# A second buffer for normed key tiles, first and last tile normed by halves, turns and scores placed inside the next batch's first product

## The reference, cut to what matters

```python
kvx = jnp.einsum('bsi,oi->bso', cond, w_kv_x)
kx, vx = jnp.split(kvx, 2, axis=-1)
kx = _ln(kx.reshape(b, sc, g, d), kxln_w, kxln_b)      # mean and variance over d = 128
vx = vx.reshape(b, sc, g, d)
xout = _gqa(qx, kx, vx).reshape(b, s, nh * d)          # softmax(qx kx / sqrt(d)) vx
```

## Time and profile before

| | |
|---|---|
| median of 3 runs | 2918.24 us (2917.55 to 2921.14) |
| the profiled execution | 2916.87 us, span of its instructions 2915.1 us |
| mean granted TensorE clock | 0.969 of full |
| busy over the span | PE 92%, PEld 75%, DVE 61%, ACT 52%, POOL 16% |

### The profile page before, as it was taken

How to read it: one execution, slowest core, us unless ns; L and a number is a source line. 1 busy time by engine, 2 the same in 40 slices (tenths; PEclk the granted TensorE clock), 3 DMA queues, 4 the chain that set the end, 5 groups by cost and what they waited for, 6 DMA issues and landing times.

```text
span 2915.1 us, 38394 instructions
## 1 busy us (share of the span) xinstructions
PE 2690.7 (92%) x13446; PEld 2184.2 (75%) x13446; DVE 1785.1 (61%) x4709; ACT 1503.8 (52%) x2907; POOL 462.5 (16%) x376
## 2 busy tenths in 40 slices
PE   6869999999999999999999999989998889868999
PEld 5767778778787787787787786768876678756887
DVE  6745536537437447356356366568768776557997
ACT  6934424425326336235244344336675467846776
POOL 3401102002002002011011020004332222011111
PEclk9978999999999999999999999999999899988999
DMA  3425002002012011021020021335666542529996
GB/s 119 131 73 184 25 8 88 11 24 81 2 42 63 3 56 48 4 70 32 5 79 23 9 82 42 101 140 148 178 182 174 137 104 58 176 87 386 373 372 238
DMA packets 247006, 303.07 MB, mean 104 GB/s; under 512 B 144024, under 2 KB 165144, under 8 KB 233504
## 3 DMA queue, kind: packets, MB, share of 16 engines
q1 hardware_dynamic: 244016, 296.36, 32.0%
q0 software_dynamic: 2800, 4.27, 0.6%
HBM read 259.48 MB, written 46.98 MB: 105 GB/s over the span
## 4 chain that ended last, share of the span: by engine, by line
PE 75%; DVE 11%; ACT 6%; DMA 3%; issue 2%; SPq 2%; POOL 1%; POOLq 0%; DVEq 0%; ACTq 0%
PE ps L103 18%; PE ps L105 18%; PE ps L104 18%; PE ps L734 5%; PE ps L716 3%; PE ps L753 3%; PE ps L783 2%; DVE lnw L1958 1%; DVE zz L1961 1%; DVE cv L1925 1%; PE ps L774 1%; POOL lnw L1080 1%; DVE lnw L831 1%; DMA ca<-cat_d 1%; PE ps L481 1%
## 5 line engine op out<-in xcount | busy, mean ns | idle before, releaser
L1080 POOL TENSOR_TENSOR lnw<-lnw,half 128x8 f32<-128x8 f32 (+1 forms) x104 | 170.7, 1642 | 1451.5 <-DVE lnw L836 1451.5
L103 PE MATMUL ps<-cnh,pth 128*128 128x512 f32 (+1 forms) x832 | 332.5, 400 | 13.6 <-ACT kn L962 13.6
L103 PE MATMUL ps<-whf,cth 128*128 128x512 f32 (+1 forms) x832 | 336.7, 405 | 6.9 <-DVE ctl L538 3.5
L105 PE MATMUL ps<-whf,ctl 128*128 128x512 f32 (+1 forms) x832 | 327.5, 394 | 0.0
L104 PE MATMUL ps<-wlf,cth 128*128 128x512 f32 (+1 forms) x832 | 327.0, 393 | 0.0
L105 PE MATMUL ps<-cnh,ptl 128*128 128x512 f32 (+1 forms) x832 | 326.6, 392 | 0.0
L104 PE MATMUL ps<-cnl,pth 128*128 128x512 f32 (+1 forms) x832 | 326.4, 392 | 0.0
L962 ACT ACTIVATE pr<-ps,lnw 128x128 f32<-128x128 f32 (+1 forms) x384 | 144.6, 457 | 164.0 <-DVE lnw L855 164.0
L2399 DVE TENSOR_TENSOR ml<-mr,mh 128x2048 fp32r<-128x2048 f32 x90 | 203.5, 2288 | 32.4 <-ACT mh L2343 32.4
L952 DVE TENSOR_SCALAR pc<-ps,sm 128x512 f32<-128x512 f32 x64 | 48.1, 751 | 283.6 <-PE ps L105 283.6
L1024 ACT ACTIVATE xo<-ps 128x128 f32<-128x128 f32 x64 | 17.8, 278 | 370.7 <-PE ps L783 370.7
(11 more groups left out here) (332 smaller groups left out, 6103.3 us busy)
## 6 DMA issues: line engine op xcount, KB each, us to landing
mr<-in_moe SPq DMA_DIRECT2D x90, 1024.0 KB, 6.8
ctr<-in_ctxt SPq DMA_DIRECT2D x96, 256.0 KB, 2.9
pr<-in_ctxn SPq DMA_DIRECT2D x96, 256.0 KB
wr<-in_wqkv SPq DMA_DIRECT2D x64, 256.0 KB, 2.9
wvf<-in_wattn SPq DMA_DIRECT2D x12, 1024.0 KB, 5.0
ca<-cat_d SPq DMA_DIRECT2D x16, 512.0 KB, 4.1
qk_d<-cv SPq DMA_DIRECT2D x32, 256.0 KB, 3.2
wr<-in_wz SPq DMA_DIRECT2D x32, 256.0 KB, 3.1
```

What stands on the lines that cost most here:

```text
L103: pe.matmul(dst, lh, rh, start=first, stop=False)
L105: return pe.matmul(dst, ll, rh, start=False, stop=last)
L1080: po.tensor_tensor(rs[0:w, s, :], nv[0:w, s, :], half[0:w, 0:8], ALU.pow).then_inc(kx_rs, 1)
```

## The change

- `kn` and `kn0` now alternate: odd tiles go to `kn`, even ones to `kn0` (`kn_of`), and `kn_free` waits for the turn of the tile before the last.
- Tiles 0 and 12 of a batch are treated by halves of 4 heads: TensorE reports the first part of the product (`kx_half`), VectorE takes the statistics of each half by itself, GpSimd makes two powers of 4 columns for them.
- `nmr` is made of heads 0 to 3 only, those that ScalarE norms (`kx_nmr_dv`).
- A turn waits for ScalarE's heads before its first four transposes and for VectorE's before the other four, instead of for both before the first.
- On TensorE the turn of tile 10 moves between the two parts of tile 12's product, and the turn of tile 12 and the last score piece move into the first part of the next batch's tile 0; the turn of tile 12 lay ahead of it.
- On VectorE, step i does the norm of tile i-2, the split `cnl` of tile i-1, then the statistics of tile i-1. At the batch's end the order is: statistics of tile 12, first half; norm of 11; `nmr` of 12; second half; `cnl` of 11; norm of 12. The first-half statistics of the next tile 0 come right behind the softmax's maximum.
- On ScalarE the norm of tile 12 comes ahead of the copies `kf` of tile 11.

```diff
@@
+        def in_halves(n):
+            return n % 13 in (0, 12)
+        def kn_of(n):
+            return kn if n % 13 % 2 else kn0
...
@@ kx_pe
                 elif i == 0:
                     pe.wait_ge(kn_ac, n)
-                    pe.wait_ge(kn_dv, n)
...
             for part in parts:
+                if part == 1 and i == 0 and b > 0:
+                    pe.wait_ge(kn_dv, n)
                 for c in chunks:
...
+                if part == 0 and chunks[-1] == 3 and in_halves(n):
+                    f.then_inc(kx_half, 1)
@@ kx_turn_pe
-            src = kn if i else kn0
-            pe.wait_ge(kn_ac, n + 1)
-            pe.wait_ge(kn_dv, n + 1)
+            src = kn_of(n)
             for p in range(2):
+                pe.wait_ge((kn_ac, kn_dv)[p], n + 1)
@@ s3_pe
-                    kx_pe(pe, n)
+                    kx_pe(pe, n, (0,))
+                    if i == 12:
+                        kx_turn_pe(pe, n - 2)
+                    kx_pe(pe, n, (1,))
...
-                    if i > 1:
+                    if 1 < i < 12:
                         kx_turn_pe(pe, n - 2)
                 kx_turn_pe(pe, 13 * b + 11)
                 for w in range(3):
                     score_pe(pe, b, 0, w)
+                if b + 1 < NB:
+                    kx_pe(pe, 13 * b + 13, (0,), (0, 1))
                 kx_turn_pe(pe, 13 * b + 12)
                 if b + 1 < NB:
-                    kx_pe(pe, 13 * b + 13, (0,), (0, 1))
+                    kx_pe(pe, 13 * b + 13, (0,), (2, 3))
                 score_pe(pe, b, 0, 3)
                 if b + 1 < NB:
-                    kx_pe(pe, 13 * b + 13, (0,), (2, 3))
                     kx_pe(pe, 13 * b + 13, (1,))
@@ kn_free
             elif i > 1:
-                eng.wait_ge(k_turned, 2 * (n - 1) + 2)
+                eng.wait_ge(k_turned, 2 * (n - 2) + 2)
+
+        def kx_nmr_dv(dv, n):
+            i = n % 13
+            w, s = TILES[i][1], i % 4
+            dv.wait_ge(kx_rs, kx_stat_of(n, 0))
+            dv.scalar_tensor_tensor(nmr[0:w, s, 0:4], mv[0:w, s, 0:4, 0], -1.0, rs[0:w, s, 0:4],
+                                    ALU.mult, ALU.mult).then_inc(kx_nm, 1)
@@ s3_dv
                     n = 13 * b + i
+                    if i > 2:
+                        kx_norm_dv(dv, n - 2)
+                    if i < 12:
+                        split_ctxn_dv(dv, n - 1)
                     if i > 1:
                         kx_stats_dv(dv, n - 1)
-                    if i > 2:
-                        kx_norm_dv(dv, n - 2)
-                    split_ctxn_dv(dv, n - 1)
                     if i + 2 < 13 or (i == 11 and b + 1 < NB):
                         split_ctxt_dv(dv, n + 2)
+                kx_stats_dv(dv, 13 * b + 12, (0,))
                 kx_norm_dv(dv, 13 * b + 11)
-                kx_stats_dv(dv, 13 * b + 12)
+                kx_nmr_dv(dv, 13 * b + 12)
+                kx_stats_dv(dv, 13 * b + 12, (1,))
+                split_ctxn_dv(dv, 13 * b + 11)
                 kx_norm_dv(dv, 13 * b + 12)
...
+                if b + 1 < NB:
+                    kx_stats_dv(dv, 13 * b + 13, (0,))
                 t_rinv = {0: rinv_dv(dv, b, 0)}
                 split_ctxn_dv(dv, 13 * b + 12)
...
                     if g == 0 and b + 1 < NB:
-                        kx_stats_dv(dv, 13 * b + 13)
+                        kx_stats_dv(dv, 13 * b + 13, (1,))
+                        kx_nmr_dv(dv, 13 * b + 13)
                     p_low_dv(dv, b, g, (0, 1))
@@ s3_ac
                 kx_norm_ac(ac, 13 * b + 11)
+                kx_norm_ac(ac, 13 * b + 12)
                 k_out_ac(ac, 13 * b + 11)
-                kx_norm_ac(ac, 13 * b + 12)
                 k_out_ac(ac, 13 * b + 12)
```

More of the change, by code:

```diff
@@ L588, in s1b_ac @@
                     split_ctxt_ac(ac, 1)
+        kx_half = sem("kx_half")
         kx_done, kx_var, kx_rs, kx_nm = sem("kx_done"), sem("kx_var"), sem("kx_rs"), sem("kx_nm")
@@ L599, in p_exp_of, with kx_half_of, kx_stat_of @@
             return m + 1 + (m + 7) // 8
+        def in_halves(n):
+            return n % 13 in (0, 12)
+        def kx_half_of(n):
+            return 2 * (n // 13) + 1 + n % 13 // 12
+        def kx_stat_of(n, h):
+            b, i = divmod(n, 13)
+            return 15 * b + (1 + h if i == 0 else i + 2 + (h if i == 12 else 0))
+        def kn_of(n):
+            return kn if n % 13 % 2 else kn0
         KSET = [(0, 2, 6)[(i + 2) % 3] for i in range(13)]
@@ L823, in s3_pe, with kx_stats_dv @@
                         xo_pe(pe, m - 1)
-        def kx_stats_dv(dv, n):
+        def kx_stats_dv(dv, n, halves=(0, 1)):
             b, i = divmod(n, 13)
             w, s = TILES[i][1], i % 4
+            lo, hi = 4 * halves[0], 4 * halves[-1] + 4
             src = bank(KSET[i], 2)[0:w, :]
-            dv.wait_ge(kx_done, n + 1)
-            for g in range(8):
+            if halves == (0,):
+                dv.wait_ge(kx_half, kx_half_of(n))
+            else:
+                dv.wait_ge(kx_done, n + 1)
+            for g in range(lo, hi):
                 t = vs(dv.bn_stats(bns[0:w, s, g, :], src[:, 128 * g:128 * g + 128]))
             dv.wait_ge(dv_step, t)
-            for g in range(8):
+            for g in range(lo, hi):
                 t = vs(dv.bn_aggr(mv[0:w, s, g, :], bns[0:w, s, g, :]))
             dv.wait_ge(dv_step, t)
-            dv.tensor_scalar(nv[0:w, s, :], mv[0:w, s, :, 1], 1e-5, None, ALU.add).then_inc(kx_var, 1)
+            dv.tensor_scalar(nv[0:w, s, lo:hi], mv[0:w, s, lo:hi, 1], 1e-5, None, ALU.add).then_inc(kx_var, 1)
         def kn_free(eng, n):
@@ L841, in kn_free @@
             if i == 0 and b > 0:
-                eng.wait_ge(k_turned, 2 * (n - 13) + 2)
+                eng.wait_ge(k_turned, 2 * (n - 1) + 2)
             elif i == 1 and b > 0:
-                eng.wait_ge(k_turned, 2 * (n - 2) + 2)
                 eng.wait_ge(p_turned, 32 * b - 4)
             elif i > 1:
-                eng.wait_ge(k_turned, 2 * (n - 1) + 2)
+                eng.wait_ge(k_turned, 2 * (n - 2) + 2)
[5 more added lines that the diff above has]
+                                    ALU.mult, ALU.mult).then_inc(kx_nm, 1)
         def kx_norm_dv(dv, n):
@@ L852, in kx_norm_dv @@
             src = bank(KSET[i], 2)[0:w, :]
[L853 to L856, removed]
+            dst = kn_of(n)
+            if not in_halves(n):
+                kx_nmr_dv(dv, n)
+            dv.wait_ge(kx_rs, kx_stat_of(n, 1))
             kn_free(dv, n)
@@ L897, in s3_dv @@
         def s3_dv(dv):
-            kx_stats_dv(dv, 0)
+            kx_stats_dv(dv, 0, (0,))
+            kx_stats_dv(dv, 0, (1,))
             for c in range(2):
@@ L904, in s3_dv @@
             split_ctxt_dv(dv, 2)
+            kx_nmr_dv(dv, 0)
             kx_norm_dv(dv, 0)
@@ L957, in kx_norm_ac @@
             src = bank(KSET[i], 2)[0:w, :]
-            dst = kn if i else kn0
+            dst = kn_of(n)
             ac.wait_ge(kx_nm, n + 1)
@@ L1078, in s3_po @@
                 w, s = TILES[n % 13][1], n % 13 % 4
-                po.wait_ge(kx_var, n + 1)
-                po.tensor_tensor(rs[0:w, s, :], nv[0:w, s, :], half[0:w, 0:8], ALU.pow).then_inc(kx_rs, 1)
+                if in_halves(n):
+                    for h in range(2):
+                        po.wait_ge(kx_var, kx_stat_of(n, h))
+                        po.tensor_tensor(rs[0:w, s, 4 * h:4 * h + 4], nv[0:w, s, 4 * h:4 * h + 4], half[0:w, 0:4],
+                                         ALU.pow).then_inc(kx_rs, 1)
+                else:
+                    po.wait_ge(kx_var, kx_stat_of(n, 1))
+                    po.tensor_tensor(rs[0:w, s, :], nv[0:w, s, :], half[0:w, 0:8], ALU.pow).then_inc(kx_rs, 1)
         x = sb("x", [128, 4, 512])
@@ L2006, in program @@
         o_high, o_low, gr_silu = Again(self_exp, 4), Again(self_p, 4), Again(self_turned, 4)
-        og_out, og_turned, gated = Again(kx_var, 104), Again(kx_rs, 104), Again(kx_nm, 104)
+        og_out, og_turned, gated = Again(kx_var, 120), Again(kx_rs, 120), Again(kx_nm, 104)
         ot_high, ot_low, out_done = Again(kx_done, 104), Again(kn_ac, 104), Again(kn_dv, 104)
```

## The result

The changed kernel takes 3009.64 us (median of 4 runs, 3008.52 to 3011.85); the kernel before, 2919.69 us (4 runs). The ratio is 1.0309, with a 95% interval of 1.0291 to 1.0326: 90 us slower. The forecast was 2988 with a range of 2970 to 3012. The mean granted clock is 0.965 for 0.969.

The account below looks back on a forecast made before the run. TensorE was taken to bound the kernel, with at most 41.9 us of waits removable. Terms 59.4 + 14.4 - 7 + 3 = +69.8 on 2916.9 gave 2986.7, or 2988 us on the median's scale; range 2970 to 3012.

Parts of the forecast that it names:

- The loop: Mid-batch chain statistics, power, `nmr`, ScalarE's norm, `cnh`, `cnl`, next statistics: 7.17 us against TensorE's step of 6.35; +59.4 us.
- the likeliest case: Whole kernel: the loop binds as worked out, about 2970 to 3004 us by itself; chance 0.83.
- the clock's case: The loop binds and TensorE's clock falls at two idles per batch: 24 us more, 3012 us; chance 0.08.
- The waits: TensorE's waits at the transposes for ScalarE's normed keys: some 104 us in place of 28.3 us.
- The batch's end: From the turn of tile 9 to the first turn of the probabilities: 23.0 us for 21.2; +14.4 us in all.
- tile 0: Next batch's first tile normed by halves: product with the values starts 1.0 us earlier per batch; 7 us gained in all.
- The clock: TensorE at 1.2 GHz after the 3.6 us idle at tile 10, mostly hidden: 0.4 us per batch, +3 us.
- The first rival: Mid-batch chain doesn't bind, so tiles 10 and 11 are normed early: 23 us gained, 2895 us; chance of faster 0.06.
- the wait of 2.50: TensorE's idle before the turn of tile 11 in the kernel before, 2.50 us, put down to the one buffer `kn`.

## Why the prediction was right, and where a term was short

**The loop** was the cause, as argued: two runs take it away (turns at 6.35, 2902.62 and 2891.19), one puts it alone into the kernel before (3047.18), and one shortens it (6.64). **Its length** was short by one piece. I took the power at 1.64 us from the earlier trace rows, since there nothing holds it up. In the new order `ctl` (L538) starts right behind the statistics, 0.17 before the power, and the power takes 2.01. The run with `ctl` moved has 1.64 and a round of 7.17, so the 0.37 is shown to be that. Per batch the powers of tiles 1 to 8 and 10 grow by 0.37 and that of tile 9, beside a short `ctl`, by 0.11: 9 x 0.37 + 0.11 = 3.44. In batch 0 the first one stays at 1.64 (253.60 below), where the forecast had 2.01, so that this batch grows by 3.44 - 2 x 0.37 = 2.70: 7 x 3.44 + 2.70 = 26.8. My bound for a loop was 0.05, a seventh of what was missing. The earlier trace rows has a power of 2.01, which I took for an oddity of batch 0.

**The range** held by luck. By itself the likeliest case reached to 3004, and 3009.64 lies above that; the stated 3012 came from the clock's case, which did not come about. The waits agree by chance as well (101.3 us, forecast 104): I had taken the whole excess of a loop for idle. In the run with `ctl` moved, whose loop is the 7.17 of the forecast, a turn shows 0.60 of the excess of 0.82 as idle, and the waits are 45.0 us at even and 33.4 us at odd tiles, 78.4 in all. The longer power brought them back up.

**The batch's end** and **tile 0** were sized right: 23.26 for 23.0, of which 0.34 is the longer power of tile 10 (7.54 for 7.2), and 5.26 for 5.3. The power of four columns, put at 1.1 in proportion between one and eight, takes 1.00.

**The clock**, put in with 3 us, did fall after the idle of 3.63 at tile 10 (matmuls of 0.63 at 544.34), and the loss vanishes in the wait for tile 11, which is left with 0.22 where I had forecast 2.0. So that term is near nothing.

What the prediction did not see is that the clock fell in the kernel before as well. It took batch 1 as the example, where the waits left the clock at its upper level. In batch 0 of the same trace the product with the values, behind the same wait of 1.95, falls to the lower one:

```profile
337.23 0.50 PE L103 MATMUL ps<-cnh,pth 128*128 128x512 f32 x1 [1.95 <-ACT kn L962]
...
339.31 0.63 PE L104 MATMUL ps<-cnl,pth 128*128 128x512 f32 x1
```

The granted clock of the first 4.7 us of this product is 0.64 to 0.66 in batches 0, 3 and 5 and 1.00 in the four others that have a next batch, and each of the three loses 1.6 us. In the changed kernel it is 1.00 in all seven: a gain of 4.8 that stands in no term.

**The sum** with these is 59.4 + 14.4 - 7 + 26.8 - 4.8 = 88.8. Of the 95.0 between the two spans, 88.2 have arisen by the last batch's first product with the values (1865.8 for 1777.7). The other 6.8 lie behind it, in work that the change does not touch and that takes 1137.4 to 1150.1 us in the ten profiled executions.

**The other cases.** The first rival put the kernel without the loop at 2895; the two runs without it give 2902.62 and 2891.19. I had myself put the wait of 2.50 down to the one buffer `kn`, and that was wrong. The rival's rule from the Trainium skill, "Perfetto Trace Analysis", section "Identifying Performance Opportunities" (a repeated gap as a sign of missing buffers), does not hold for the 2.50 here: with the second buffer alone it stays at 2.49. By the trace it repeats because ScalarE's norm of tile 11 stands behind its copies of tile 10; no run turned these two round, but with the turn of tile 10 moved forward the wait falls to 1.3. The clock's case came true at no place of the changed kernel that counts (in batches 2 and 6 some 0.2 and 0.6 us were not hidden), but in the run without halves.

## What to carry to other kernels

When a change reorders one engine's steps, write down for each instruction what it now stands behind, on its engine and, through the waits, on the others, and look whether the chain returns to its own start one step later; if it does, its length has to be below the step of the busiest engine. Price each link with the neighbours that it gets in the new order, and look for a wait or a fall of the clock in every batch, not in one. A repeated wait can come from the order of a queue and not from a missing buffer: look first at what stands ahead of the releasing instruction. The good parts of this change (halves, moved turns, second buffer) are worth 31 us once `cnl` goes behind the statistics.

## What the hardware showed that was not expected

GpSimd's power is held up by a VectorE instruction that is in flight when it starts and takes both its operands from SBUF, as `ctl` and `cnl` do. With a `ctl` of 0.68 us begun 0.17 before, it takes 2.01; with one of 0.42 begun 0.18 before, 1.75; without, 1.64. The half power takes 1.38 beside `cnl` (549.10 above) and 1.00 without. In each case it is as if the power began about 0.13 before the VectorE instruction ends (an estimate from these numbers).

Two operands alone are not enough. `ptl` reads one of its two from PSUM (`ps`), and beside it the half power of the next tile 0 takes 1.01:

```profile
560.35 1.28 DVE L928 TENSOR_TENSOR ptl<-ps,pth 128x512 fp32r<-128x512 f32 x2
...
560.44 1.01 POOL L1125 TENSOR_TENSOR lnw<-lnw,half 128x4 f32<-128x4 f32 x1 [2.19 <-DVE lnw L864]
```

It is so in all seven batches that have a next one, and in the kernel before the power of 8 columns takes 1.65 at this place.

Begun later, an instruction of the first kind did no harm in batch 0 of the changed kernel:

```profile
253.60 1.64 POOL L1129 TENSOR_TENSOR lnw<-lnw,half 128x8 f32<-128x8 f32 x1 [16.14 <-DVE lnw L864]
...
253.90 0.69 DVE L538 TENSOR_TENSOR ctl<-ctr,cth 128x512 fp32r<-128x512 f32 x1 [0.38 <-ACT cth L546]
```

Here `ctl` starts 0.30 after the power and runs 0.69, and the power still takes 1.64. The Trainium skill, "GPSIMD Engine Reference", section "Key points", says that GpSimd shares its SBUF interfaces with VectorE and contends with instructions that have two SBUF inputs. The trace agrees: `ctl` and `cnl` have two such inputs (2.01 and 1.38), `ptl` has one (1.01). What counts in these cases is the instruction in flight at the start.
